# A recurrence kernel: the state's matrix product one step later, and another order of work on GpSimd

## What is computed

```python
xn = layernorm(x)
proj = xn @ in_proj_w.T                    # gate 4096, conv input 6144, dt 64
xBC = silu(causal_conv(proj_conv, taps=4)) # x: 64 heads x 64, B and C: 8 groups x 128
for t in range(L):                         # per batch and head
    state = state * dA[t] + (dt[t] * x[t]) outer B[t]
    y[t] = state @ C[t]
y = y + x * D
yn = y * rsqrt(mean(y*y over each group of 512) + eps) * norm_weight * silu(gate)
s = yn @ out_proj_w.T
out = x + s * silu(xn @ W.T + bias + lora_out)
```

## Time and profile before

| | us |
|---|---|
| median of 3 runs | 1863.41 |
| lowest and highest | 1862.56, 1866.68 |
| the profiled execution | 1867.85 |
| its span, first to last instruction | 1866.0 |

### The profile page before, as it was taken

One profiled execution on the slowest core, in us unless ns is written; L12 is line 12 of the kernel. 1 busy time (PEld: TensorE's weight loads), 2 busy tenths in 40 slices (PEclk: granted clock), 3 DMA queues, 4 the chain that ended last, 5 costly groups with the idle time before them and its releaser, 6 DMA issues.

```text
span 1866.0 us, 31464 instructions
## 1 busy us (share of the span) xinstructions
PE 1733.9 (93%) x10792; PEld 1375.5 (74%) x10792; DVE 1480.7 (79%) x1839; ACT 1021.8 (55%) x2715; POOL 1307.5 (70%) x1255
## 2 busy tenths in 40 slices
PE   8979989999998999999888998999999899999986
PEld 5757767777777877777777787777777777777865
DVE  7858788787878878787877887878788787878886
ACT  4555555655555565555645655465555546555544
POOL 6537668686767858676797857669585766958576
PEclk9989999999999999999999999999999999999989
DMA  8445545555454555455775654546355454635445
GB/s 265 145 143 167 168 142 172 143 165 149 147 169 147 170 151 160 144 155 167 221 243 177 180 163 150 164 146 189 110 177 156 145 163 146 187 112 166 150 139 184
DMA packets 322415, 304.76 MB, mean 163 GB/s; under 512 B 88272, under 2 KB 255568, under 8 KB 322256
## 3 DMA queue, kind: packets, MB, share of 16 engines
q1 hardware_dynamic: 321216, 302.60, 54.1%
q10 hardware_dynamic: 1040, 0.16, 0.0%
HBM read 246.57 MB, written 56.10 MB: 162 GB/s over the span
## 4 chain that ended last, share of the span: by engine, by line
PE 75%; DVE 9%; issue 8%; ACT 4%; POOL 2%; DMA 2%; SPq 1%; ACTq 0%; DVEq 0%; POOLq 0%
PE ps_conv L1345 9%; PE ps_conv L1348 8%; PE ps_y L1507 6%; PE ps_conv L1351 6%; PE ps_s L1537 6%; PE ps_gate L1345 5%; PE ps_out L1348 5%; PE ps_out L1345 5%; PE ps_gate L1348 5%; PE ps_y L1512 5%; PE ps_out L1351 4%; PE ps_gate L1351 4%; DVE xc L914 2%; PE ps_conv L1352 2%; ACT dtx L831 2%
## 5 line engine op out<-in xcount | busy, mean ns | idle before, releaser
L914 DVE SCALAR_TENSOR_TENSOR xc<-ps_conv,convw_sb,xc 128x511 f32<-128x511 f32 (+2 forms) x576 | 430.4, 747 | 221.5 <-ACT xc L693 207.9
L1276 POOL TENSOR_TENSOR rstd_col<-mean_square,half 128x1 f32<-128x1 f32 x128 | 111.6, 872 | 435.8 <-ACT mean_square L813 435.6
L1049 DVE TENSOR_TENSOR_SCAN decay<-decay,eye 128x1024 f32<-128x1024 f32 x125 | 293.6, 2349 | 0.0
L813 ACT ACTIVATE mean_square<-ps_g,eps 128x1 f32<-128x1 f32 x128 | 33.4, 261 | 453.0 <-PE ps_g L1338 453.0
L1255 POOL TENSOR_TENSOR cpre<-cpre,xc 128x1024 f32<-128x1024 f32 x112 | 267.9, 2392 | 0.0
L831 ACT ACTIVATE dtx<-x_tok,prefix_dt 128x64 f32<-128x64 f32 x1024 | 257.4, 336 | 8.6 <-DMA b_tok<-turned_d 8.6
L1345 PE MATMUL ps_conv<-xn_hi,wconv_hi 128*128 128x512 f32 x768 | 258.5, 460 | 0.0
L1348 PE MATMUL ps_conv<-xn_hi,wconv_lo 128*128 128x512 f32 x768 | 214.4, 402 | 0.0
L1537 PE MATMUL ps_s<-xw,b_tok 128*128 128x512 f32 x224 | 125.4, 643 | 95.4 <-issue 75.7
L1507 PE MATMUL ps_y<-decay,dtx 128*64 128x128 f32 x1984 | 191.5, 280 | 5.0 <-DVE decay L1069 5.0
L1345 PEld LDWEIGHTS ps_conv<-xn_hi,wconv_hi 128*128 128x128 f32 x768 | 143.5, 197 | 56.6 <-issue 31.3
(11 more groups left out here) (233 smaller groups left out, 3911.9 us busy)
## 6 DMA issues: line engine op xcount, KB each, us to landing
decay<-decays_d SPq DMA_DIRECT2D x125, 512.0 KB, 5.1
cpre<-rows_d SPq DMA_DIRECT2D x112, 512.0 KB, 3.8
turned_d<-squares SPq DMA_DIRECT2D x512, 80.0 KB, 2.0
stage<-w_in_t SPq DMA_DIRECT2D x32, 1024.0 KB, 5.2
x_tok<-turned_d SPq DMA_DIRECT2D x128, 256.0 KB, 3.2
stage<-w_out_t SPq DMA_DIRECT2D x16, 1024.0 KB, 5.4
stage<-w_in_t SPq DMA_DIRECT2D x32, 256.0 KB, 3.2
b_tok<-turned_d SPq DMA_DIRECT2D x128, 64.0 KB, 3.8
```

The source lines that it names most:

```text
L914: e.scalar_tensor_tensor(acc[:, d:], ps[:, 0:BLK - d], convw_sb[:, tile, TAPS - 1 - d:TAPS - d], acc[:, d:], ALU.mult, ALU.add).then_inc(S ...
L1049: e.tensor_tensor_scan(d, d, eye8[:, :, :].rearrange("p h i -> p (h i)"), 0.0, ALU.mult, ALU.add).then_inc(scanned(i)[0], 1)
```

## The change

Two things move; no operation is added or removed.

1. TensorE does the state's product of a chunk in the next turn, as the first thing behind that chunk's mixing products, and no longer behind the gate's tile in the chunk's own turn. The choice between before and behind the convolution tile falls away with it.
2. On POOL the root moves from the start of the turn to behind the second sum of squares, and `xw` from behind the splits to behind `skip`. `cpre` now follows the splits directly.

```diff
--- before.py
+++ after.py
@@ -1269,11 +1269,6 @@
             for i in range(N + DRAIN):
                 m, u = i - 1, i - DRAIN
                 f = finished(i)
-                if u >= 0:
-                    col = slice(u % 2, u % 2 + 1)
-                    w.wait_ge(S["var2"], u + 1)
-                    w.wait_ge(S["osum"], u - 1)
-                    e.tensor_tensor(rstd_col[:, col], mean_square[:, col], half[:, :], ALU.pow).then_inc(S["rstd2"], 1)
                 if i < N:
                     g, at = divmod(i, NCH)
                     left = BATCH * GROUPS - 1 - g
@@ -1289,8 +1284,6 @@
                         split_conv_bc(g + 1, range(KT))
                     if at == 6 and left:
                         split_gate(g + 1, (2, 3))
-                if i < N and i % NCH < NCH - 1:
-                    scale_x(i)
                 if i < N and i % NCH > 0:
                     left_of_state(i)
                 if 0 <= m < N:
@@ -1300,6 +1293,12 @@
                     w.wait_ge(S["sum1"], m + 1)
                     w.wait_ge(S["mm_ssq"], m)
                     e.tensor_tensor(square_sum[:, :], square[:, 0:P], square[:, P:2 * P], ALU.add).then_inc(S["sum2"], 1)
+                if u >= 0:
+                    col = slice(u % 2, u % 2 + 1)
+                    w.wait_ge(S["var2"], u + 1)
+                    w.wait_ge(S["osum"], u - 1)
+                    e.tensor_tensor(rstd_col[:, col], mean_square[:, col], half[:, :], ALU.pow).then_inc(S["rstd2"], 1)
+                if 0 <= m < N:
                     if cm < NCH - 2:
                         new, dec = state[(group(m) + cm) % 2], state[(group(m) + cm + 1) % 2]
                         w.wait_ge(S["state"], inner(m))
@@ -1322,6 +1321,8 @@
                     e.tensor_tensor(turns(skip), xc[nb % 2][:, 0:XT, block_cols(i % NCH)],
                                     dskip_sb[:, gi * XT:(gi + 1) * XT].unsqueeze(2).to_broadcast([P, XT, P]),
                                     ALU.mult).then_inc(S["skip"], 1)
+                if i < N and i % NCH < NCH - 1:
+                    scale_x(i)
                 if i < N and i % NCH == 0:
                     edges(group(i))
                 if f is not None and not on_vector(f):
@@ -1512,6 +1513,12 @@
                                 mixed = e.matmul(y_h, before[:, h * HD:(h + 1) * HD], c_left[:, h, :], start=False,
                                                  stop=True, skip_group_check=True)
                     mixed.then_inc(S["mm_in"], 1)
+                if 0 <= m < N and cm < NCH - 1:
+                    w.wait_ge(S["pt"], len(RATES))
+                    w.wait_ge(landed_tok[m % 2], 32 * (m // 2 + 1))
+                    w.wait_ge(S["xw"], inner(m))
+                    w.wait_ge(S["state"], inner(m - 1) if m > 0 else 0)
+                    e.matmul(ps_s[:, :], b_tok[m % 2][:, :], xw[:, :], start=True, stop=True).then_inc(S["mm_u"], 1)
                 if i < N:
                     w.wait_ge(S["silu"], max(conv_no(i // CPB, t) for t in (XT, XT + 1)) + 1)
                     w.wait_ge(S["var2"], u if u >= 0 else 0)
@@ -1526,16 +1533,7 @@
                     conv(conv_early(i))
                 for k in gated(i):
                     gate(k)
-                late_first = i < N and conv_early(i) is None and conv_late(i) is not None
-                if late_first:
-                    conv(conv_late(i))
-                if i < N and i % NCH < NCH - 1:
-                    w.wait_ge(S["pt"], len(RATES))
-                    w.wait_ge(landed_tok[i % 2], 32 * (i // 2 + 1))
-                    w.wait_ge(S["xw"], inner(i))
-                    w.wait_ge(S["state"], inner(m) if m >= 0 else 0)
-                    e.matmul(ps_s[:, :], b_tok[i % 2][:, :], xw[:, :], start=True, stop=True).then_inc(S["mm_u"], 1)
-                if i < N and conv_late(i) is not None and not late_first:
+                if i < N and conv_late(i) is not None:
                     conv(conv_late(i))
```

## The result

The changed kernel took 1992.45 us (median of 4 runs, 1990.66 to 1993.52) against 1864.01 us for the kernel before (4 runs, 1862.56 to 1866.68): 1.0686 times as long, 95% interval 1.0668 to 1.0705. The forecast was 1879 us, with 1900 as the upper end of its range. Its direction held and its size did not: +0.9% was forecast and +6.9% measured. The profiled execution took 1993.52 us with a span of 1991.7, 125.7 us more than the 1866.0 of before.

A forecast was written before the change was run, and what follows sets the result against it. It took TensorE, 93% busy, and the ring of engines behind each mixing product as the bound. Groups at +1.0 us (12 with clock fall) or +2.0 (2 without) gave +16 us, other steps 0: 1879 us, ends 1857 and 1896, 8-in-10 range 1850 to 1900.

The forecast's parts named there:

- The removed idle: TensorE ahead of the state product: 95.4 us of idle goes, 5.3 us + 1.6 us a group at most.
- The product at 0.86 us: TensorE between mixing product and ps_g: the state product occupies 0.86 us, delaying mean_square by that in most steps.
- the upper bound (1.2): State product among half-width products: 1.2 us if joining them costs a refill of 0.2 each side, +9 us in all.
- Positions 7 and 0: Steps whose number modulo 8 is 7 or 0: lengths 13.1 (+2.1) and 10.6 (-0.9).
- Position 1: Steps numbered 1 modulo 8: out_sum starts at 12.9; length 18.35 (+0.1) with the clock's fall, 17.75 (+1.1) without.
- Hidden: xw last in POOL's step: ends some 11.5 us after the step's start, wanted 1.9 us after the next; no cost.
- Position 3: Steps numbered 3 modulo 8: scan starts at 2.4, cpre behind it, out_sum at 8.95; length 13.8, +0.1.
- Position 4: Steps numbered 4 modulo 8: TensorE's own length stays above the end of the matrix, so change 0.
- The rest at 0, within 5: First group, two groups with closing steps, and last steps: gains and losses set at 0 together, within 5 us.
- The lock falls the other way: Rival, chance 0.15: cpre goes before the waiting scan, 2.4 us later at position 3, also at 6; 1900 us.
- The wait moves only: Rival, chance 0.03: xw arrives after the mixing product and TensorE waits ahead of ps_g; 1 us each gives 1990 us.
- Partly faster: Rival, chance 0.11: position 1 profits, output product released at about 11.5, clock holds, length 16.3; 1850 us.

The follow-up runs named there:

- TensorE's part alone: Against the kernel before: state's product moved behind the next turn's mixing products, POOL's order as before; 1817.12 us, ratio 0.973.
- the last run: Against the 1785.73 us kernel (POOL order cpre, root, splits, xw, sums): root moved behind xw, directly ahead of the sums; 1845.45 us, ratio 0.9883.
- `xw` in the middle: Against the changed kernel: xw back behind the splits, ahead of cpre, root still behind the sums; 2002.11 us, ratio 1.0724.

## Why the prediction was wrong in size

Of the 7.7 us by which a group grew, 1.0 had been forecast. The missing 6.7 are 2.4 at position 1, 2.5 at position 3, 0.5 at position 4 and 1.3 at the other five, where the price of the product is most of it. Point by point, by its own steps.

- **The removed idle.** Right. "That is 5.3 us + 1.6 us a group at most": TensorE's part alone took 3.3 us off a group after paying for the product, and position 1 alone got 4.1 us shorter. (The idle in its own rows is 3.1 + 2.0 = 5.1 us, not 5.3; nothing hangs on the difference.)
- **The product at 0.86 us.** Mis-sized. `mean_square` starts 3.50 us behind the mixing product at position 7, and 2.30 once the product is out of the way: 1.20 us. The merged row gave the distance of the product's own two instructions; that the full-width product joins half-width ones at a price was in the text as the upper bound (1.2), and that bound is the measured value. The 0.2 us "each side" behind it stood on no row; the runs show 0.34 for both sides together. It also lengthens positions 2, 6 and 7 by 0.3 each and takes as much from the gain at 5: 1.2 us a group of the missing 6.7.
- **Positions 7 and 0.** Right, 13.39 for 13.1 and 10.66 for 10.6. The chain square, sums, root, `out_sum`, matrix is as forecast, the 0.3 is the product's.
- **Position 1.** The mechanism was right ("out_sum starts at 12.9"), three sizes in it were not. The first split starts at 5.03 us and not 3.6: 1.02 through the edges (the run with the edges ahead of `xw` took this much back), which the change moved behind `xw` and for which the forecast had "Hidden" as its only word, and 0.4, the rest, which I put down to the product's price. The first split took 2.03 us for 1.29, since the scan was running (0.74). Together 15.1, measured 14.93. The idle is 4.77 us where 3.2 was forecast, and the step is 20.5 instead of 18.35.
- **Position 3.** The step that failed: "the scan starts at 2.4, cpre behind it". The scan did start at 2.38, but `cpre` 0.03 us ahead of it, so the scan took 4.50 us instead of 2.28 and y came 2.2 us late: `out_sum` starts at 10.99 where 8.95 was forecast, and the step is 16.25 us where 13.8 was. My estimate of 1.4 for when DVE wants its scan was the earlier trace rows of a step in which TensorE's idle shifted everything; without that idle DVE has three taps in front of it and is ready at 2.46. Worse, the order hardly mattered: with the scan ahead, DVE's `last` waits for `cpre` instead. The forecast knew the lock between two instructions and priced it as one delay for POOL's sums; it did not ask what stands behind the scan on DVE. By the Trainium skill (SBUF — State Buffer, "Who interferes with whom") the order of issue decides which of two such instructions blocks; the trace agrees, with 0.03 us in one kernel and 0.15 us the other way in the next. The clock's fall there was forecast only for position 1. It costs the step some 0.6 us: in the kernel with the edges ahead of `xw`, the output product takes 3.95 us up to the next mixing product at position 3 where the clock holds (5 of 13 steps; the mixing matrix sets the end), and 4.5 in the changed kernel where it falls.
- **Position 4.** "0" was +0.54. TensorE's part alone has 11.77 (+0.18); the other 0.36 come with a wait of 0.47 us for `out_sum` ahead of the output product's first weights. I had compared the end of the matrix with the step's length there, not the release of the output product.
- **The rest at 0, within 5.** +27.5 us. The groups with the closing steps and the tail have POOL fuller than a regular group, and lose more and not less; moving the root alone gave 5.0, 9.7 and 7.1 us back of the 4.8, 11.3 and 11.4 that the first group, steps 57 to 66 and the end had grown by. I had counted the removed idle there and not the new wait.

**The rivals.** *The lock falls the other way* is what happened, with 0.15 for it and +1.5 us a group; at position 3 alone it cost more than that, and at position 6 nothing (the scans there last 2.69 us on the mean, but TensorE's own 14.49 covers it). *The wait moves only* gave 1990 us, near the measured 1992, but its mechanism is absent: two of 112 products wait for `xw`, 2.3 us in all. That its time fits is luck, and no evidence for its mechanism. *Partly faster* failed by its own criterion, when POOL gets to its first sum at position 1: 13.1 us.

Each unknown was bounded by itself, and all the errors of size have the same sign. Most of them, though not the product's, meet in one step: the forecast treated the root's new place as a fixed addition of 1.3 us behind the square, and `out_sum` now waits for whatever stands ahead of the root in POOL's queue, contention included.

**Still open.** How the part of the last run's 60 us outside positions 1, 3 and 4 divides between fence and root; where the 0.4 us at position 1 that I put down to the product come from; and why `xw` in the middle costs 5 us in steps 57 to 66 (167.2 instead of 162.3).

## What to carry to other kernels

A tiny instruction that others wait for belongs at the point where its input is ready, ahead of every queue that can grow; here 0.55 us, placed behind two sums instead of ahead of them, cost 89 us. Where two engines lock each other out, look at what stands behind the locked instruction on both engines, not only at who goes first. And a wait that looks like pure loss (POOL standing at `mean_square`) can be what keeps the other engine's long instruction undisturbed: before removing it, see what starts in its place.

## What the runs showed of the hardware

- A scan of 128x1024 on VectorE takes 2.28 us alone, and longer by nearly what the POOL instruction that started ahead of it has left to run: 4.50 us behind 2.38 us of `cpre`, 2.84 behind 0.72. Two chains of such instructions take turns: scan 2.34, `cpre` 4.39, `last` 2.20 instead of 0.17.
- The state product of two full-width instructions takes 1.20 us between half-width products and some 0.86 elsewhere.
- The same idle of TensorE can be followed by a short or a long stretch at the lower clock. At position 1 of the changed kernel, with 4.8 us of idle in every regular step, the granted clock was at 0.50 for 3.4 us in 7 of 12 steps and for 6.8 us in 5; the output product took 4.5 and 4.9 to 5.3 us. With the edges ahead of `xw` and 3.8 us of idle it was 6.8 us in 10 of 12 steps. In both kernels all the long stretches began 0.9 us or more ahead of the product's start, and all the short ones at its start or behind it. So one step's loss to the clock says little; count it over all steps.
